# Local attention layers: probabilities normalised by GpSimd in their rows, values as the stationary operand, queries left unscaled

## The reference

```python
def _layer(x, wqkv, qs, ksc, wo, lg, lb, w1, b1, w2, b2):      # 8 heads of 64, windows of 64
    h = shift_token(x)
    q, k, v = jnp.split(h @ wqkv, 3, axis=-1)                   # then split into heads
    q = l2norm(q) * qs
    k = l2norm(k) * ksc
    q, k = rotary_xpos(q, k)                                    # q*cos*scale + rotate_half(q)*sin*scale, k with 1/scale
    o = local_attention(q, k, v)                                # softmax over own and preceding window, times 8
    x = x + o @ wo
    h = layernorm(shift_token(x)) * lg + lb
    a, g = jnp.split(h @ w1 + b1, 2, axis=-1)
    return x + (a * gelu(g)) @ w2 + b2
```

## Time and profile before

| | |
|---|---|
| median of 3 runs | 2219.2 us (2218.24 to 2221.23) |
| the profiled execution's own time | 2221.09 us |
| its span, first to last instruction | 2219.4 us |
| mean granted TensorE clock | 0.959 |
| first and last cast of line 1003 | 731.7 and 2047.6 us |

### The profile page before, as it was taken

One profiled execution on the slowest core, in us unless ns is written; L12 is line 12 of the kernel. 1 busy time (PEld: TensorE's weight loads), 2 busy tenths in 40 slices (PEclk: granted clock), 3 DMA queues, 4 the chain that ended last, 5 costly groups with the idle time before them and its releaser, 6 DMA issues. The chain is left out here.

```text
span 2219.4 us, 52419 instructions
## 1 busy us (share of the span) xinstructions
PE 2010.5 (91%) x20476; PEld 1350.0 (61%) x20476; DVE 1806.2 (81%) x3455; ACT 1623.4 (73%) x3312; POOL 1380.4 (62%) x2090
## 2 busy tenths in 40 slices
PE   2999999999995489999999999999999999999971
PEld 1566666666663366676676676666666666666641
DVE  1788988888883468889989889896998998998746
ACT  1577777777774368888888888786878888888745
POOL 3598888888875665556556556554655655665403
PEclk9899999999998589999999999999999999999985
DMA  1001010010100111100100100111010011011014
GB/s 42 1 16 30 16 30 16 16 30 16 30 11 10 42 33 33 35 19 19 36 19 19 36 19 19 30 38 29 19 32 22 19 30 24 19 28 26 19 39 114
DMA packets 50548, 59.92 MB, mean 27 GB/s; under 512 B 8145, under 2 KB 43393, under 8 KB 48257
## 3 DMA queue, kind: packets, MB, share of 16 engines
q1 hardware_dynamic: 50304, 56.58, 10.2%
HBM read 17.90 MB, written 8.39 MB: 12 GB/s over the span
## 5 line engine op out<-in xcount | busy, mean ns | idle before, releaser
L982 POOL TENSOR_TENSOR b_part_b<-b_raw,b_tabs 128x256 f32<-128x256 f32 x512 | 432.3, 876 | 297.3 <-ACT b_raw L1041 262.7
L991 POOL TENSOR_TENSOR b_qk<-b_qk,b_part_b 128x1024 f32<-128x1024 f32 x128 | 332.2, 2596 | 271.1 <-DVE b_qk L1141 263.9
L1141 DVE TENSOR_TENSOR b_qk<-b_raw,b_tabs 128x512 f32<-128x512 f32 x256 | 296.7, 1199 | 0.1
L1242 PE MATMUL b_work<-b_w_high,b_h_high 128*128 128x512 f32 x384 | 191.1, 498 | 30.6 <-DVE b_h_low L1131 19.2
L473 POOL TENSOR_SCALAR_AFFINE_SELECT a_probs<-a_probs 128x256 f32<-128x256 f32 x512 | 203.3, 409 | 0.0
L1316 PEld LDWEIGHTS b_work<-b_v_even,b_pT 128*64 128x64 f32 x2048 | 136.9, 138 | 78.1 <-issue 72.6
L584 DVE TENSOR_REDUCE a_qpack<-a_pa 128x2 f32<-128x1024 f32 (+2 forms) x128 | 143.7, 1122 | 44.0 <-PE a_pa L655 41.4
L1062 ACT ACTIVATE b_probs<-b_sb,b_neg_max 128x128 f32<-128x128 f32 x512 | 147.9, 383 | 41.4 <-DVE b_neg_max L1163 41.0
L422 POOL TENSOR_TENSOR a_idle<-a_idle 128x1 f32<-128x1 f32 x432 | 86.6, 200 | 146.9 <-ACT a_probs L516 85.2
L1030 ACT ACTIVATE b_sq<-b_work 128x1024 f32<-128x1024 f32 x128 | 131.7, 1029 | 54.4 <-PE b_work L1244 43.7
L1068 ACT COPY b_pT<-b_work 128x512 f32<-128x512 f32 x256 | 154.4, 603 | 23.0 <-PE b_work L1306 23.0
(11 more groups left out here) (211 smaller groups left out, 5518.1 us busy)
## 6 DMA issues: line engine op xcount, KB each, us to landing
b_v_even<-b_v SPq DMA_DIRECT2D x32, 528.0 KB, 4.4
b_v_even<-b_v SPq DMA_DIRECT2D x32, 396.0 KB, 5.8
a_x_in<-in_L_attn_x SPq DMA_DIRECT2D x16, 256.0 KB, 3.2
a_x_again<-in_L_attn_x SPq DMA_DIRECT2D x16, 256.0 KB, 3.5
x_scratch<-a_x SPq DMA_DIRECT2D x16, 256.0 KB, 2.5
out<-c_y SPq DMA_DIRECT2D x4, 1024.0 KB, 5.4
b_w_raw<-in_L_ffn_wqkv SPq DMA_DIRECT2D x2, 768.0 KB, 4.3
b_tabs<-tab SPq DMA_DIRECT2D x2, 512.0 KB, 4.2
```

The source lines that it names most:

```text
L982: last = pool.tensor_tensor(part_b[:, x, :].rearrange("p (h d) -> p h d", d=DH)[:, :, lo:lo + DH // 2], raw[:, i % 2, x, :].rearrange("p ( ...
L991: pool.tensor_tensor(qk[:, i], qk[:, i], part_b[:], ALU.add).then_inc(c_made, 1)
L1141: last = dve.tensor_tensor(qk[:, i, x, :].rearrange("p (h d) -> p h d", d=DH), raw[:, i % 2, x, :].rearrange("p (h d) -> p h d", d=DH), ta ...
L1242: pe.matmul(x, h_high[:, t], w_high[:, cols], start=True, stop=False)
```

## The change

- `scale` now multiplies k alone, 512 elements a row. q is transposed unscaled as soon as `rope_add` is done. In its place `row_max` keeps raw maxima and a new VectorE product of eight elements a row, raw_max times rs, makes neg_max, and `exp` takes rs as a scale for each row beside the bias. rs is kept for two sequences.
- `rope_cos` reads q and k from their PSUM banks and frees them; ScalarE still copies them into `raw` for `rope_sin`, and `raw_made` tells of it.
- The ones behind the values go. New on VectorE is `sums` for a pair: a reduction over the probabilities of two heads (1024 elements a row, from SBUF) and a reciprocal of the eight sums. New on GpSimd is `norm` for a head: the probabilities (512 elements a row) times that reciprocal, in place. `p_turn` waits for it. `divide` is gone.
- `values` works on a pair: the values are stationary, the transposed probabilities move (64 columns), and the outputs come out with features as rows, where `out` needs them; `o_turn` is gone and `copy_o` reads the bank of `values`.
- The semaphore of the shifted values is one per slot, `h` on GpSimd waits until the last projection is filled and not until it is read, one fill of ones is dropped, and `ORDER` is written anew, with other banks.

The code, cut to its core:

```diff
 def rope_add(l, b, i, slot):
     n = seq(l, b) * TT + i
     pool.wait_ge(b_made, n + 1)
-    pool.wait_ge(a_made, n + 1)
+    until_read(pool, "project_k", i, l, b)
     pool.tensor_tensor(qk[:, i], qk[:, i], part_b[:], ALU.add).then_inc(c_made, 1)
...
+def norm(l, b, h, slot):
+    pool.wait_ge(den_made, seq(l, b) * PAIRS + h // 2 + 1)
+    pool.tensor_tensor(probs[:, h % 4], probs[:, h % 4],
+                       rden[:, h, :].rearrange("p (i a) -> p i a", a=1).to_broadcast([P, TT, P]), ALU.mult).then_inc(normed, 1)
...
     for i in range(TT):
         last = act.activation(probs[:, h % 4, i, :], bank_of[which][:, a, i * P:(i + 1) * P], ACT.Exp,
-                              bias=neg_max[:, slot, h, i:i + 1])
+                              bias=neg_max[:, slot, h, i:i + 1], scale=rs[:, slot, i, 0, h:h + 1])
...
 def rope_cos(l, b, i, slot):
-    until_read(dve, "project_k", i, l, b)
-    for x in range(2):
-        last = dve.tensor_tensor(qk[:, i, x, :].rearrange("p (h d) -> p h d", d=DH),
-                                 raw[:, i % 2, x, :].rearrange("p (h d) -> p h d", d=DH),
+    dve.wait_ge(raw_made, seq(l, b) * TT + i + 1)
+    for x, name in enumerate(("project_q", "project_k")):
+        from_bank, read = to_read(dve, name, i, l, b)
+        dve.tensor_tensor(qk[:, i, x, :].rearrange("p (h d) -> p h d", d=DH),
+                          from_bank.rearrange("p (h d) -> p h d", d=DH),
...
 def row_max(l, b, p, slot):
-    dve.tensor_reduce(neg_max[:, slot, 2 * p:2 * p + 2, :], bank_of[which][:].rearrange("p a (i k) -> p a i k", i=TT),
-                      AX, ALU.max, negate=True).then_inc(maxed, 1)
+    step(dve.tensor_reduce(raw_max[:, p], bank_of[which][:].rearrange("p a (i k) -> p a i k", i=TT), AX, ALU.max, negate=True))
+    dve.tensor_tensor(neg_max[:, slot, 2 * p:2 * p + 2, :], raw_max[:, p],
+                      rs[:, slot, :, 0, 2 * p:2 * p + 2].rearrange("p i a -> p a i"), ALU.mult).then_inc(maxed, 1)
...
+def sums(l, b, p, slot):
+    step = steps("sums", p, l, b)
+    until_read(dve, "scores", p, l, b)
+    two = slice(2 * p % 4, 2 * p % 4 + 2)
+    step(dve.tensor_reduce(den[:, p], probs[:, two], AX, ALU.add))
+    dve.reciprocal(rden[:, 2 * p:2 * p + 2, :], den[:, p]).then_inc(den_made, 1)
...
 def p_turn(l, b, h, slot):
+    pe.wait_ge(normed, seq(l, b) * HEADS + h + 1)
+    x, full = to_fill(pe, "p_turn", h, l, b)
...
+def values(l, b, p, slot):
     for w in range(WINS):
+        for a in range(2):
+            h = 2 * p + a
+            last = pe.matmul(x[half_rows(a), w * WIN:(w + 1) * WIN], (v if w % 2 else v_even)[:, slot, w // 2, h, :],
+                             pT[:, h % 4, w * WIN:(w + 1) * WIN], start=True, stop=True)
```

More of the change, by code:

```diff
@@ L751 @@
 WINS = T // WIN
-VW = DH + 2
 SEQS = DEPTH * B
-OWN_STEPS = {"newton": 3, "divide": 1, "variance": 2, "rstd": 3, "weights_ffn": 1}
+OWN_STEPS = {"newton": 3, "row_max": 1, "sums": 1, "variance": 2, "rstd": 3, "weights_ffn": 1}
 ORDER = [
[L758 to L787, removed]
@@ new lines @@
+    (1, "norm", 0), (2, "out", 1), (1, "p_turn", 0, "w1"), (1, "row_max", 2), (0, "copy_v", 0), (1, "norm", 1),
+    (2, "out", 2), (1, "exp", 2), (1, "exp", 3), (1, "copy_p", 0), (1, "sums", 1), (2, "out", 3), (2, "residual", 0),
+    (1, "p_turn", 1, "x"), (0, "rope_sin", 1), (1, "norm", 2), (1, "exp", 4), (0, "square_sums", 1), (1, "copy_p", 1),
+    (1, "exp", 5), (0, "project_q", 2, "w0"), (0, "project_k", 2, "w1"), (0, "rope_add", 1), (0, "square", 2),
+    (0, "raw_q", 2), (2, "stat_turn", 0, "x"), (1, "values", 0, "o"), (2, "variance", 0), (1, "norm", 3),
@@ new lines @@
+    (0, "rope_cos", 3), (2, "gate", 0, "x"), (2, "gelu", 0), (2, "gate", 1, "o"), (2, "gate", 2, "w1"),
+    (0, "square_sums", 3), (1, "row_max", 3), (2, "hidden", 0, "w0"), (0, "limit", 0), (2, "gelu", 1),
+    (2, "hidden", 1, "o"), (2, "gelu", 2), (2, "product", 0), (2, "product", 1), (1, "norm", 4), (0, "seed", 0),
+    (1, "exp", 6), (2, "hidden", 2, "x"), (1, "exp", 7), (2, "product", 2), (0, "newton", 0), (0, "turn_q", 0, "w1"),
+    (2, "down", 0, "o"), (2, "down", 1), (1, "p_turn", 4, "w0"), (0, "turn_q", 1, "x"), (0, "scale", 0),
@@ L788 @@
+    (0, "rope_add", 2), (0, "rope_sin", 3), (0, "scale", 1), (1, "norm", 5), (0, "copy_q", 0), (1, "copy_p", 4),
+    (0, "turn_q", 2, "w1"), (0, "copy_q", 1), (0, "project_v", 3, "w0"), (2, "down", 2), (1, "sums", 3),
+    (0, "rope_add", 3), (0, "copy_q", 2), (0, "scale", 2), (2, "result", 0), (0, "scale", 3),
 ]
@@ L1023, in copy_v @@
                 x, read = to_read(act, "project_v", i, l, b)
-                act.copy(v[:, slot, i, :, 0:DH], x.rearrange("p (h d) -> p h d", d=DH)).then_inc(read, 1)
+                act.copy(v[:, slot, i], x.rearrange("p (h d) -> p h d", d=DH)).then_inc(read, 1)
             def square(l, b, i, slot):
@@ L1216, in _ @@
                            rope_cos=rope_cos, limit=limit, newton=newton, scale=scale, row_max=row_max,
-                           divide=divide, residual=residual, variance=variance, rstd=rstd_, normalise=normalise, product=product, result=result))
+                           sums=sums, residual=residual, variance=variance, rstd=rstd_, normalise=normalise, product=product, result=result))
         @block.tensor
```

111 lines of the change are left out of this document (54 added, 57 removed).

## The result

The changed kernel is slower: 2250.78 us median against 2218.83 beside it, 31.95 us more, a ratio of 1.014 with a 95% interval of 1.0126 to 1.0153. One of its four executions took 3128.77 us at a granted clock of 0.558; the median counts it (without it: 2250.05), the ratio doesn't. The profiled execution took 2250.05 us, its span is 2248.3 and its mean granted clock 0.958 (0.959 before).

A forecast was written before the change was run, and what follows sets the result against it. TensorE was taken to set the period of 41.7 us before; after the change, a loop through TensorE, VectorE and GpSimd of 25.1 + 10.5 + 7.8 = 43.4, 51 us more in all. Forecast 2270 us, own range 2222 to 2325, widened to 2172 to 2325.

The forecast's parts named there:

- TensorE's loss of work: TensorE, per period: the 16 transposes of the outputs go, 1.68 us less.
- the loop: First projection, third sums, GpSimd's chain to rope_add 3, newton, low, next first projection: 43.4 us a period, chance 0.57.
- Leg A: First projection to the end of the third sums, through TensorE and VectorE with waits: 25.1 us.
- Leg B: GpSimd alone, after the third sums to rope_add 3: two norms, two rope_add, one rope_sin and gaps, 10.5 us.
- Leg C: VectorE behind rope_add 3, from newton's last step over scalings, fourth sums and result to low: 7.8 us.
- The sum: Period of the middle stage: 25.1 + 10.5 + 7.8 = 43.4 us, +1.7 on 41.7, over 31 distances 51 us.
- Products of eight elements: VectorE, behind the maxima: counted as waiting for GpSimd; if exempt, the period would be 1.3 us shorter.
- VectorE's 32.4 busy: VectorE's busy time per period after the change, net -5.1 us.
- GpSimd's forecast of 34: GpSimd's busy time per period with eight new products of 512 elements, 9.6 us in all: 34 us.
- First rival, TensorE keeps the period: Newton and scalings fall between GpSimd's instructions, TensorE's queue sets the period: 40.0 us, time 2167, chance 0.24.
- Second rival, the short loop: Waits are short and norm 7 lets low pass: period 41.0 to 41.8 us, time 2197 to 2222, chance 0.14.
- Third rival, the clock: TensorE's granted clock falls in each period, between the scalings: 96 us more, time 2366, chance 0.05.

The follow-up runs named there:

- one-element run: Changed kernel with GpSimd's norm on one element a row in place of 512, all waits kept: 2176.82 us, ratio 0.9806.
- three moves: Changed kernel, rope_add 2 in front of norm 4 and behind rstd, norm 7 waiting for low, norm 1 for the second maximum's product: 2183.01 us.
- rope_add 2 moved: Changed kernel with GpSimd's rope_add 2 in front of norm 4, waiting for rstd's steps: 2216.87 us, ratio 0.9986.
- both moves: Changed kernel with rope_add 2 in front of norm 4 and waiting for rstd, and norm 7 waiting for low: 2199.11 us, ratio 0.9909.
- the run without the wait for rstd: Changed kernel with rope_add 2 in front of norm 4, but not waiting for rstd's steps: 2319.71 us, ratio 1.0448.

## Why the prediction came out as it did

The direction and the mechanism were right: a time of 2250.8 in the forecast's own range, for the reason given. The size came out as close as it did partly by luck, since errors of the legs cancelled. By its steps:

- **TensorE's loss of work** happened: 20476 matmuls became 19964, 16 fewer for each of 32 sequences. In the windows TensorE is busy 39.59 for 40.80, and 38.56 in the one-element run and with three moves; so 1.2 to 2.2 less, around the 1.68 that was counted. It was worth nothing while the loop set the period.
- **Leg A**, 25.1 forecast, measured 25.8. The way to the first maximum takes 3.38 for 3.1. Of the 22.45 from there, four meetings cost 0.39, 0.85, 0.21 and 0.42 (each duration less the 0.17 that it takes in the open) = 1.9, where 2.25 was taken. The waits for ScalarE, 0.64 + 0.22 for exponentials, 0.23 for a copy and 0.49 for a seed = 1.6, had been priced at 0.15. That was the leg's mis-sized term: the exponentials were costed as work beside other work, though the sums wait for the last of them.
- **Leg B**, 10.5 forecast, measured 9.7. A norm in the open takes 1.04, below both ends (1.2 to 1.4). Two of them are 0.3 of the difference; the rest is in the gaps, since norm 4 followed the sums at once.
- **Leg C**, 7.8 forecast, measured 7.3, from newton's last step over two scalings to low, in the order given. Low met norm 7 and lost 0.85 where 1.2 was counted, again mostly the norm's length (norm 7's row of 1.49 has a wait of its own in it, for the scaling in front of low); the scaling beside h's cast took 0.69 and lost 0.05, where 0.3 was counted.
- **The sum**, 43.4 forecast, measured 42.78. Of the forecast's 1.65 above 41.70 two thirds came, and 32 us in place of 51. Legs B and C were 1.3 too long in the forecast, A 0.7 too short. The forecast took all 31 distances as periods and left filling and draining at nothing, at worst 10 either way; 26 were, and what the other five, the start and the end took more and less came to 0.5 in sum.
- **Products of eight elements.** The prediction left open whether they wait. They do: 0.17 in the open, 0.38 to 1.02 in the changed kernel and 2.03 in a run. The Trainium skill, "SBUF — State Buffer", section "SBUF: two separate sides", makes no exception for size, and the trace agrees. The forecast had counted them in.
- **VectorE's 32.4 busy** was the sum of its work without the waiting; 36.83 with it, 33.40 where the norms were cut. GpSimd's forecast of 34 was too high (30.16), for the cosine products from the banks freed it as well: a quarter of rope_sin has a mean of 732 ns, for 876 before and 915 in the run with cosine products from SBUF again.
- **First rival, TensorE keeps the period.** It was said to decide as soon as newton's third step stood before rope_add 3. In the run with rope_add 2 moved newton is clear of that addition (which there ends before it), and the period was 41.61, still the loop's. Only with low and the eight-element product freed too does the period come near 40.0. So the rival's condition was incomplete; its leg A would have needed its low end as well.
- **Second rival, the short loop** (41.0 to 41.8), is where the kernel stands with rope_add 2 moved (41.61) or with both moves (40.97), not as it was made.
- **Third rival, the clock.** It stayed at 1.00 in the window, with TensorE idle 3.2 of 42.78. Nothing of the loss is the clock's. In the run without the wait for rstd it did fall, to 0.96 in most periods, and a period there is 44.80 at 0.96 (1039.48 to 1084.28) as at 1.00 (904.93 to 949.73): while the loop sets the period, that much of the clock cost nothing.

Left open: the period of 40.52 still lies 0.5 above the 40.0 that TensorE's queue was given. By its rows low and TensorE's own queue arrive at the first projection together there; which of TensorE's waits holds the period was not tried. Nor was it tried why the end of the stage, behind the last cast, grew by 7.4.

## What to carry to other kernels

Where VectorE's instructions wait for GpSimd's, as here, work given to GpSimd costs more than its own time: what counts is which VectorE instruction of the critical loop asks just after a GpSimd one has begun. List these meetings from the timeline (a short instruction with a long duration, ending with a GpSimd one), and remove them one at a time, with a wait on GpSimd for the VectorE instruction that it would block, where GpSimd has room. After each move look again, because a GpSimd instruction that is moved can hold up the next VectorE instruction instead, as limit and two of the eight-element products were here.

## What the runs showed that was not expected

- An instruction with one operand from SBUF waits too: limit, 128 x 64, lasts 0.18 in the open, 1.10 beside norm 5 and 2.41 beside rope_add 3. The Trainium skill, "SBUF — State Buffer", section "Who interferes with whom", counts this kind of operation (a tensor with scalars) among those that can enter a two-port mode and so contend with GpSimd; the trace agrees. The prediction had sorted the instructions by two operands and left limit out, though a row of its own showed the kind: line 1193 in the earlier trace rows, 0.55 long, adds a constant to one operand from SBUF.
- Three waits added to the engine with the most new work, and one of its tasks moved, with no work removed, took 67.8 us off.
- A scale from SBUF lengthened ScalarE's exponentials by 104 ns on the mean (487 against 383 in the page's row of the kernel before; the 379 of the earlier trace rows is a median); ScalarE's busy time in a period rose by 2.7, which over 32 exponentials is 85 ns each.
